# Macaron block with a gated delta-rule recurrence: the second half of the layers one group late, in halves of 256 tokens, inside the next group's recurrence

## What is computed

```python
x = x + 0.5 * ffn0(layernorm(x))          # silu(x wg) * (x wu), times wd; hidden width 768
x = x + delta_attention(layernorm(x))     # 16 heads, key width 64, value width 128
x = x + 0.5 * ffn0(layernorm(x))
x = x + 0.5 * shift_ffn(layernorm(x))     # mixes each token with the one before it
x = x + block_attention(layernorm(x))     # 16 heads of 16, causal inside blocks of 64 tokens
x = x + 0.5 * shift_ffn(layernorm(x))
# delta_attention, per head and token t, after projections, a causal convolution of 4 taps and silu:
S = a_t * (S - b_t * k_t (k_t S)) + k_t v_t ;  o_t = S q_t
# then an RMS norm of o_t and the product with Wo
```

## Time and profile before

| | us |
|---|---|
| median of 3 runs (9527.74 to 9530.57) | 9528.12 |
| the profiled execution, its time | 9529.48 |
| its span | 9527.7 |
| TensorE busy | 7091.6 (74%) |
| VectorE busy | 4742.1 (50%) |
| GpSimd busy | 2896.9 (30%) |
| ScalarE busy | 2594.3 (27%) |
| mean granted TensorE clock | 0.846 of 2.4 GHz |

### The profile page before, as it was taken

How to read it: one execution, slowest core, us unless ns; L and a number is a source line. 1 busy time by engine, 2 the same in 40 slices (tenths; PEclk the granted TensorE clock), 3 DMA queues, 4 the chain that set the end, 5 groups by cost and what they waited for, 6 DMA issues and landing times. The chain is left out here.

```text
span 9527.7 us, 151688 instructions
## 1 busy us (share of the span) xinstructions
PE 7091.6 (74%) x55840; PEld 4885.9 (51%) x55840; DVE 4742.1 (50%) x9325; ACT 2594.3 (27%) x5122; POOL 2896.9 (30%) x3781
## 2 busy tenths in 40 slices
PE   6777777767787777877778777787777777777777
PEld 3644546445464454645546455464554645546455
DVE  5445454454544545445454454545545455464553
ACT  2223132231322313223132231322313223132231
POOL 2315133251322513225132251322513225132251
PEclk8888888888888888888888888888888888888888
DMA  1101001010010100101001010010100101001010
GB/s 48 48 3 25 30 10 48 3 27 28 10 48 3 29 26 10 48 3 34 21 10 48 3 34 21 10 48 3 34 21 10 48 3 34 21 10 48 3 35 3
DMA packets 376009, 225.64 MB, mean 24 GB/s; under 512 B 336880, under 2 KB 353392, under 8 KB 366960
## 3 DMA queue, kind: packets, MB, share of 16 engines
q1 hardware_dynamic: 375152, 214.71, 7.5%
HBM read 155.95 MB, written 58.72 MB: 23 GB/s over the span
## 5 line engine op out<-in xcount | busy, mean ns | idle before, releaser
L538 DVE SCALAR_TENSOR_TENSOR SC<-SC,CW 128x512 f32<-128x512 f32 x1536 | 1281.9, 835 | 255.8 <-DVEq L536 170.0
L1097 PE MATMUL PS<-CST,SC 128*128 128x128 f32 x2432 | 494.7, 351 | 951.8 <-PEq L1105 520.2
L768 POOL TENSOR_TENSOR RSTD<-VAR,NHALF 128x2 f32<-128x2 f32 x192 | 133.8, 697 | 3009.0 <-POOLq L767 3009.0
L1097 PEld LDWEIGHTS PS<-CST,SC 128*128 128x128 f32 x2432 | 351.1, 177 | 1227.1 <-issue 1210.4
L839 POOL TENSOR_TENSOR WO<-WO 128x30 f32<-128x30 f32 (+14 forms) x960 | 581.9, 606 | 262.9 <-POOLq L853 126.3
L1094 PE MATMUL PS<-S,KQ 64*64 64x128 f32 x8192 | 659.2, 278 | 0.0
L842 POOL TENSOR_TENSOR WO<-WO 128x30 f32<-128x30 f32 (+14 forms) x960 | 613.8, 639 | 136.4
L1094 PE MATMUL PS<-XT,WV 128*128 128x512 f32 x1024 | 524.7, 652 | 115.0 <-PEq L1205 77.1
L862 POOL TENSOR_TENSOR FR<-MS,NHALF 128x8 f32<-128x8 f32 x128 | 210.0, 1641 | 1265.7 <-POOLq L861 1265.7
L1094 PE MATMUL PS<-XT,WQK 128*128 128x512 f32 x1024 | 576.2, 699 | 0.0
L1094 PE MATMUL PS<-WV,SC 64*64 64x128 f32 x8192 | 531.8, 280 | 41.9 <-PEq L1296 41.9
(11 more groups left out here) (159 smaller groups left out, 13423.5 us busy)
## 6 DMA issues: line engine op xcount, KB each, us to landing
WV<-in_wv SPq DMA_DIRECT2D x16, 2048.0 KB, 12.8
WO<-in_wo SPq DMA_DIRECT2D x16, 2048.0 KB, 7.5
WQK<-in_wq SPq DMA_DIRECT2D x16, 1024.0 KB, 4.8
WQK<-in_wk SPq DMA_DIRECT2D x16, 1024.0 KB, 6.9
cells_in<-SC SPq DMA_DIRECT2D x128, 128.0 KB, 2.8
WO<-cells_in SPq DMA_DIRECT2D x32, 512.0 KB, 3.3
cells_out<-WO SPq DMA_DIRECT2D x32, 512.0 KB, 2.6
cells_nat<-WO SPq DMA_DIRECT2D x32, 512.0 KB, 3.6
```

What stands on the lines that cost most here:

```text
L538: op = v.scalar_tensor_tensor(y, pre[:, j:j + G], CW[:, i * TAPS + j:i * TAPS + j + 1], y, ALU.mult, ALU.add)
L768: q.tensor_tensor(out=RSTD[:, 2 * k:2 * k + 2], in0=VAR[:, 2 * k:2 * k + 2], in1=NHALF[:, 0:2], op=ALU.pow).then_inc(rstd_ready, 1)
L1097: return nc.tensor.matmul(out_, in_, ident, is_transpose=True, start=True, stop=True)
```

## The change

The layers after the output projection become a generator, `tail`, on each of the four engines. It has 56 steps, marked by `yield`. They hold the layers of a whole group in two halves of HG = 256 tokens: feed-forward of both halves, first shift layer, attention of half 0, attention of half 1, second shift layer. `recurrence` of group n steps through the tail of group n - 1: 4 steps ahead of the first inverse (`FILL_FIRST`), then six in each of the 8 chunks in pairs A, B and C (`FILL`), then twice two. TensorE takes A behind `old_state` and the first `output_t`, B behind the second `output`, C behind `keys_t`. VectorE takes A and B between `right_side` and `s_update`, and C behind `mean_square`, ahead of `normalise`. GpSimd takes A and B with five columns of `substitute` behind each in chunks 0 to 2, C behind the power. ScalarE takes A ahead of the copies of `solve`'s result. The tail of group 0's recurrence works on a buffer of zeros, and the last group's tail is emitted by itself at the end.

The tail uses three PSUM banks (5 to 7) in a ring: each product claims the next (`claim` waits until its last reader has released it). The recurrence keeps banks 0 to 4; the transposed keys, `output_t`, the second inverse and the output projection (now one tile of 128 tokens at a time, `projected`, in chunks 5 to 7 and at the end) share bank 2. The second inverse is spread over chunks 3 and 4 in four passes, and two places of the first one wait for both copies together.

In attention the weights are no longer divided by their sum on GpSimd; `scaled` on VectorE divides the weighted sums. Two x buffers (`XS`) alternate, so VectorE's body and SyncE's loop now hold two groups. SyncE stores the late group when its tail ends and waits for the store, then loads the next x into the same buffer, then the projection weights, which before were loaded behind `chunks_done` and ahead of the rest. `chunks_done` now comes from the last tile of the output projection. The first feed-forward's layer norms take both statistics ahead of both normalisations.

```diff
+TAIL_STEPS = 56
+FILL_FIRST = 4
+FILL = 2
+
+
+def tail_ring():
+
+    order = ["x0f", "x1f"]
+    order += [f"g0{m}" for m in range(HT)] + ["d0"]
+    for m in range(HT):
+        order += [f"g1{m}"] + (["x0s"] if m == 3 else [])
+    order += ["d1", "r0s", "k0s", "v0s", "x1s", "r1s", "k1s", "v1s", "x0a"]
+    for h in range(2):
+        order += [f"q{h}0", f"q{h}1", f"va{h}", ("x1a", "x0u")[h], f"vd{h}0", f"vd{h}1", f"kt{h}0", f"kt{h}1", f"sc{h}0", f"sc{h}1"]
+        for i in range(4):
+            order += [f"pt{h}{i}", f"av{h}{i}"] + ([f"sc{h}{i + 2}"] if i < 2 else [])
+        order += [f"oa{h}", f"ao{h}"]
+    order += ["r0u", "k0u", "v0u", "x1u", "r1u", "k1u", "v1u"]
+    return {name: i % 3 for i, name in enumerate(order)}, order
+
+
+RING, RING_ORDER = tail_ring()
...
+        XB = sb("XB", 2 * NT * D)
+        XS = [XB[:, k * NT * D:(k + 1) * NT * D] for k in range(2)]
...
                     sp.dma_start(out[bass.ds(row + k * 2 * P, 2 * P), :].rearrange("(t p) d -> p t d", p=P),
-                                 v3(X[:, 2 * D * k:2 * D * k + 2 * D], 2)).then_inc(stored, 16)
+                                 v3(XS[p][:, 2 * D * k:2 * D * k + 2 * D], 2)).then_inc(stored, 16)
...
 
             def load_qkv():
                 for dst, src in ((WQ, wq), (WK, wk), (WV[:, :], wv)):
@@ -372,62 +408,67 @@
                 sp.wait_ge(a_done, 1)
                 sp.sem_inc(a_done, -1)
                 sp.dma_start(WO[:, :], wo).then_inc(wo_back, 16)
+
+            def next_qkv():
                 sp.wait_ge(chunks_done, 1)
                 sp.sem_inc(chunks_done, -1)
+                load_qkv()
...
+            load(G, 1)
+            next_qkv()
+            with sp.Fori(0, B * GROUPS // 2 - 1) as n:
+                for p in range(2):
+                    inverse_traffic()
+                    store(n * (2 * G) + p * G, p)
+                    load(n * (2 * G) + (p + 2) * G, p)
+                    next_qkv()
...
+                def hidden(h, m):
+                    ps, free = ring(f"g{h}{m}")
+                    s, u = m % 2, m % 3
+                    dve.wait_ge(tth_ready, 1)
+                    dve.sem_inc(tth_ready, -1)
+                    v.scalar_tensor_tensor(TTMP[:, s * HG:s * HG + HG], TTH[:, u * HG:u * HG + HG], 1.0, ps[:, 0:HG],
+                                           ALU.add, ALU.mult)
+                    dve.drain()
+                    v.tensor_tensor(out=THH[:, m * HG:m * HG + HG], in0=TTMP[:, s * HG:s * HG + HG], in1=ps[:, HG:G],
+                                    op=ALU.mult).then_inc(free, 1)
+                    if m == HT - 1:
+                        dve.drain().then_inc(hh_ready, 1)
+
+                def down(h):
...
+                def soft(h, i):
+                    ps, free = ring(f"sc{h}{i}")
+                    s = v3(SCB[i % 2], HB)
+                    dve.wait_ge(sc_ps, 1)
+                    dve.sem_inc(sc_ps, -1)
+                    v.tensor_tensor(out=s, in0=v3(ps, HB), in1=over(cst("amask"), HB, BLK), op=ALU.add).then_inc(free, 1)
+                    dve.drain()
+                    v.tensor_reduce(AMX[:, :], s, AX, ALU.max)
+                    dve.drain()
+                    v.tensor_tensor(out=s, in0=s, in1=each(AMX[:, :], HB, BLK), op=ALU.subtract).then_inc(sc_ready, 1)
+                    dve.drain()
+
...
+                for m in range(HT):
+                    hidden(0, m)
+                    yield
+                down(0)
+                yield
+                for m in range(HT):
+                    hidden(1, m)
+                    if m == 1:
+                        normal(0, x, TXN, txn_ready)
+                    if m == HT - 1:
+                        mix(0, 0)
+                    yield
+                down(1)
+                yield
+                normal(1, x, TXN, txn_ready)
+                yield
+                values(0, 0)
+                mix(1, 0)
+                yield
+                normal(0, x, TXN, txn_ready)
+                yield
+                values(1, 0)
+                yield
+                for h in range(2):
+                    rotate(h, 0)
+                    rotate(h, 1)
+                    if h == 0:
+                        normal(1, x, TXN, txn_ready)
+                    yield
+                    if h == 1:
+                        normal(0, x, TXN, txn_ready)
+                    yield
+                    spread(h, 0)
+                    spread(h, 1)
+                    yield
+                    yield
+                    soft(h, 0)
+                    yield
+                    soft(h, 1)
+                    sums(0)
+                    yield
+                    yield
+                    scaled(h, 0)
+                    soft(h, 2)
+                    sums(1)
+                    yield
+                    yield
+                    scaled(h, 1)
+                    soft(h, 3)
+                    sums(2)
...
+            def recurrence(p):
...
+                fill(FILL_FIRST)
                 keys(0)
...
-                        s_update(c, 1)
+                for c in range(CHUNKS):
+                    right_side(c, 0)
+                    right_side(c, 1)
+                    fill(FILL)
+                    fill(FILL)
+                    if c >= 5:
+                        projected(c - 5, XS[p])
+                    s_update(c, 0)
+                    s_update(c, 1)
...
+                    fill(FILL)
+                    if c >= 1:
+                        normalise(c - 1, 0)
+                        normalise(c - 1, 1)
+                fill(FILL)
+                fill(FILL)
+                mean_square(CHUNKS - 1)
+                normalise(CHUNKS - 1, 0)
+                normalise(CHUNKS - 1, 1)
+                projected(NT - 1, XS[p])
+                dve.drain()
 
...
+                    pool.sem_inc(qkt_ready, -1)
+                    masked_keys(0)
+                    masked_keys(1)
+                    yield
+                    yield
+                    masked_keys(2)
+                    yield
+                    yield
...
+                fill(FILL_FIRST)
                 pool.wait_ge(m_loaded, 16)
                 pool.sem_inc(m_loaded, -16)
-                cuts = (1, 14, 22, SUB - 1)
-                for c in range(CHUNKS):
-                    if c < 3:
-                        substitute(cuts[c], cuts[c + 1])
...
+                    for k in range(2):
+                        fill(FILL)
+                        if c < 3:
+                            substitute(1 + 10 * c + 5 * k, 6 + 10 * c + 5 * k)
...
+                    if c >= 1:
+                        pool.wait_ge(ms_ready, 1)
+                        pool.sem_inc(ms_ready, -1)
+                        q.tensor_tensor(out=FR[:, :], in0=MS[:, :], in1=NHALF[:, :], op=ALU.pow).then_inc(fr_ready, 1)
+                    if c < CHUNKS:
+                        fill(FILL)
 
...
+                    ps, free = ring(f"k{h}{'su'[n]}")
                     act.wait_ge(k_ps, 1)
                     act.sem_inc(k_ps, -1)
-                    ka = KA[:, k * G:k * G + G]
-                    a.activation(ka, bank(2 + k), ACT.Relu)
+                    a.activation(KA, ps, ACT.Relu).then_inc(free, 1)
                     act.drain()
-                    a.activation(ka, ka, ACT.Square).then_inc(ka_ready, 1)
+                    a.activation(KA, KA, ACT.Square).then_inc(ka_ready, 1)
...
+                def claim(name):
+                    ps, free = ring(name)
+                    if name not in RING_ORDER[0:3]:
+                        pe.wait_ge(free, 1)
+                        pe.sem_inc(free, -1)
+                    return ps
+
...
+
+                yield
+                transposed("x0f")
+                transposed("x1f")
+                yield
+                pe.wait_ge(txt_ready, 2)
+                pe.sem_inc(txt_ready, -2)
+                for m in range(HT):
+                    gate_up(0, m)
+                    yield
+                down(0)
+                yield
+                for m in range(HT):
+                    gate_up(1, m)
+                    if m == 3:
+                        transposed("x0s")
+                    yield
...
+                        ps = claim(f"kt{h}{k}")
+                        for j in range(2):
+                            for t in range(2):
+                                i = tr(ps[:, j * HG + t * P:j * HG + t * P + P], QKR[:, t * G + (2 * k + j) * P:t * G + (2 * k + j) * P + P])
+                        i.then_inc(qkt_ps, 1)
+                    yield
+                    scores(h, 0)
+                    yield
+                    scores(h, 1)
+                    yield
+                    weights_t(h, 0)
+                    yield
+                    weighted(h, 0)
+                    scores(h, 2)
+                    yield
+                    weights_t(h, 1)
+                    yield
+                    weighted(h, 1)
+                    scores(h, 3)
...
```

(93 more changed lines are left out.)

1191 lines of the change are left out of this document (682 added, 509 removed).

## The result

The changed kernel takes 9195.58 us (median of 4 runs, 9192.0 to 9202.95) against 9527.93 (9522.26 to 9530.57, 4 runs): ratio 0.9653, interval 0.9636 to 0.967. It is faster, by 3.5%. The forecast was 8892, 6.7% faster; the time lies inside the range of 8490 to 9350, 304 us above the point, between the forecast and rival (b).

The account below looks back on a forecast made before the run. TensorE was taken to bound the stretches where it is fed, handoffs the others. From a span of 9527.7 us, 833 saved over 16 groups and 195 added for the last group's lone tail gave 8890, so 8892 executed; range 8490 to 9350.

Parts of the forecast that it names:

- (b): Rival: VectorE comes late at each chunk's boundary, 3 us more a chunk, 24 a group, 9276 us; chance 0.17.
- merged stretch: Part of a group where recurrence and the late group's tail run interleaved; forecast 291 us, from 227, 54 and 10.
- front: A group's first feed-forward, projections and decay matrices; 248 us, its order left nearly alone by the change.
- waits: TensorE's waits when both streams run in its one order, counted chunk by chunk from entry to exit: 54 us a group.
- boundary: Loop overhead between groups: about 2.2 us, against 3.3 before, since one boundary of two loses its loop.
- The tail that runs alone: The last group's tail, in halves with handoffs exposed, at the end: 195 us, bounds 174 and 230.
- floor of 227: TensorE's work from recurrence through last shift layer, summed at the upper clock: 227 us a group.
- cold restarts: Lower-clock loss at a colder start, behind chunk 3's wait and at the last projection: 10 us a group.
- masked keys in chunk 6: TensorE's scores wait there for GpSimd's masked keys: 2.0 us of chunk 6's 3.9, named among the largest.
- (a): Rival: waits are mostly absorbed and the clock stays up, 29 to 32 us a group less, 8430 us; chance 0.16.
- 3 us nor 10: VectorE's slowdown beside GpSimd's substitution: 3 us, or some 10 a group if the shared port's loser fully blocks.
- (c): Rival: interrupted TensorE gets the lower clock as in attention, 98 us lost instead of 10, 10300 us; chance 0.09.

Follow-up runs that it names:

- e1_block: Changed kernel with all 56 tail steps ahead of the first inverse, so the tail is not interleaved: 10329.1 us.
- e3_warm: Changed kernel plus 46 idle TensorE products a group in front of waits for the normalised output and the returned inverse: 9088.7 us.
- e10_idle_mixed: Changed kernel plus 64 idle products a group, one ahead of each 64-row pair of a half solve: 9825.8 us.
- e5_order: Changed kernel with seven feed-forward and attention steps swapped so TensorE has other ready work before its waits: 9114.1 us.
- e4_nosub: Changed kernel without GpSimd's substitution of the second half, so the second inverse is not the inverse: 9084.6 us.
- e2_norm: Changed kernel with VectorE normalising the finished chunk between the two tail steps of pair C instead of behind both: 9208.7 us.
- e12_three_exit: Changed kernel with seven steps swapped, VectorE's exit order moved, GpSimd's slices recut, and 14 idle products at the exit only: 8985.9 us.
- e8_three_warm: Changed kernel with seven steps swapped, VectorE's exit order moved, GpSimd's slices recut, and 36 idle products a group before waits: 9020.1 us.

## Why the prediction was right or wrong

**The bound and the direction** were right, and the time lies in the range. TensorE's busy time is about what it was (7044.5 against 7091.6 us), and filling one stream's idle time with the other's work is what gains, as e1_block shows by taking it away: two thirds of its effect is idle time, one third the higher clock that comes with it. But of the prediction's own signs of being wrong one came up: TensorE's work in the merged stretch is 251.1 us, well over the 240 it named, and the granted clock 0.91, not over 0.93.

**The sum**, term by term for one group: front 247.2 against 248 (right); waits 59.1 against 54; TensorE's busy time 251.1 against 237; boundary 3.5 against 2.2. Together 561 against 541.2. Sixteen times the 20.2 us between the stores is 323. The tail that runs alone is 179 us by the method that gave 174 before, from the end of the last projection, at 8999.9, to the end of the last add at 9179.5; I had 195, so 16 us come back. 323 - 16 = 307 of the 304 us. The row of the end:

```profile
8991.03 8.88 PE L1403 MATMUL PS<-WO,VO 128*128 128x256 f32 x32 [0.87 <-PEq L1809]
```

**The mis-sized term** is TensorE's time in the merged stretch, 251 us against 237, 14 us a group; the other terms came out within 5 us. It was added up from a floor of 227 and 10 for cold restarts, three to six of them. The 10 is what failed. In this group there are nine stretches at the lower clock level, of 3.4 to 10.2 us; the last two of them and the sum of all nine:

```profile
3348.90:3355.70 6.80, 5.93 (x16) 4.97 (x17) 1.97 (x5) 1.19 (x2) 0.00 (x0) 0.50 0.01 2
3376.20:3386.40 10.20, 5.63 (x16) 4.29 (x17) 1.29 (x2) 1.20 (x2) 1.64 (x1) 0.50 0.29 89
sum 58.40, PE 48.43 PEld 41.59 DVE 15.46 ACT 11.03 POOL 10.73; mean PE 5.38 PEld 4.62 DVE 1.72 ACT 1.23 POOL 1.19
```

TensorE is busy for 48.4 of these 58.4 us. If each product takes twice its time there, 24 us are lost, 14 more than the 10, and 251.1 less 24 is the floor of 227. Over all 16 groups the mean is 249.7 us busy, 45.8 of them at the lower level. The 24 is an upper estimate, since not every product doubles (64 records of 32 x 32 take 1.73 us at 3198.40 and 1.20 at 3210.70). e3_warm supports it: the same method gives 26.4 us a group at the lower level there instead of 45.8, so some 10 us a group given back, for 21 us of idle products put mostly into waits.

The floor left out a second thing, going from one form to the other. There are 26 places of two tail steps in the merged stretch; at 0.19 us a round trip, the rows of chunk 0, they would cost 5 us, and at 0.34, e10_idle_mixed's row, 9. The clock leaves no room for 9: with its 24 us nothing is left to explain. So the change of form costs between nothing and some 5 us a group in this kernel, and these runs don't say more closely. The prediction also read 0.216 us a record off the output projection, whose own row (29.91 us for 128) gives 0.234; in the merged stretch the four projections take 30.3 us against the 27.7 of the floor, most of it in the last one, which runs in part at the lower level. Two slips had no effect: the lone tail's bound of 230 gives 9359, not 9350, as the top of the range, and attention's loss by the clock is 43% of its work (58.7 against 41), not 40.

**The waits** came out at 59 against 54, with the largest where they were named: the exit's 5.66 and 6.24, and in chunk 3 the returned blocks (L1857) and the copy of the inverse's first product (L1892):

```profile
3187.96 3.23 PE L1403 MATMUL PS<-S,KQ 64*64 64x128 f32 x32
...
3198.40 1.73 PE L1403 MATMUL PS<-WO,SC 32*32 32x32 f32 x64 [3.67 <-PEq L1857]
...
3217.27 1.15 PE L1403 MATMUL PS<-CST,KQ 64*64 64x64 f32 x32 [3.47 <-PEq L1892]
```

Chunk by chunk they are as near: entry 5.1 us against 5.1, chunk 1 2.4 against 2.0, chunk 2 7.7 against 7.3, chunk 3 8.1 against 7.5, chunk 4 4.8 against 4.9, chunk 7 5.6 against 5.4, exit 17.8 against 16. Two missed: the wait for the masked keys in chunk 6, named as one of the largest, is in no row of the merged stretch (1.8 us in all in that chunk against 3.9), and chunk 5 has 5.8 against 2.2, with 1.9 for the rows of a layer norm and 1.6 for the normalised output. No wait in the merged stretch passed 10 us. That the handoffs of adjacent steps cost time on the path, against rival (a), e5_order shows: 81 us off for reordering them alone. Such waits could be taken away by order, which I had not asked: the exit and the seven steps together were 9.8 of the 54 us.

**GpSimd.** I charged the second inverse 7.5 us in chunk 3. e4_nosub puts the whole price of the substitution at 6.9 us a group, spread beyond chunk 3. As to the shared port, VectorE's work of the merged stretch is 140.6 us (I had some 160, against 138 before), so neither 3 us nor 10 can be read out of it; leaving the substitution out took VectorE's busy time over the span only from 4897.7 to 4882.5 us, 1 us a group. In the merged stretch the rows give no sign of whole instructions blocked. In the front they do, once in each of the 16 groups: a VectorE operation with two SBUF operands that takes 0.75 us otherwise starts just behind GpSimd's copy of 1.94 us and takes 2.43, ending 0.55 us behind it. The two rows of the changed kernel:

```profile
3071.16 1.94 POOL L1055 COPY WO<-WO 128x1024 f32<-128x1024 f32 x1
...
3071.22 2.43 DVE L750 SCALAR_TENSOR_TENSOR SC<-SC,CW 128x512 f32<-128x512 f32 x1
```

The kernel before has the same (2.45 us at 2643.27). Beside the second half's copy, at 3184.82, VectorE works on operands from PSUM and takes its usual 0.69 us.

**The rivals.** (a) fell by the waits. (b) was not the mechanism: its 24 us a group were to come from VectorE being late, but only 5 us more are waits. e2_norm shows that VectorE's order is a trade, not slack. The time is nearer to (b)'s 9276 (80 us off) than to the forecast, for another reason than (b)'s, the clock. (c), the lower clock throughout, did not happen: the whole merged stretch is granted 0.91. Its rule, of the Trainium skill's page TensorE: Matmul & The Clock Gate (A second HAM failure mode: psum-queue depth-cycling), on cycling banks with small idles, is borne out in part. Chunks 1, 2 and 7 of the merged stretch, in the table of stretches:

```profile
3123.30:3150.90 27.60, 25.20 (x261) 21.89 (x260) 15.48 (x44) 5.18 (x11) 14.88 (x22) 1.00 0.01 2
3150.90:3188.00 37.10, 29.41 (x279) 23.69 (x278) 23.04 (x60) 8.81 (x15) 14.75 (x26) 1.00 0.01 4
3313.20:3344.00 30.80, 25.25 (x254) 21.88 (x252) 11.72 (x32) 5.77 (x10) 1.86 (x2) 0.89 0.00 1
```

All three cycle the same banks. Chunk 1 is idle for 2.4 us and chunk 2 for 7.7, with a wait of 3.04 us, and both keep the upper level to their end; chunk 7, idle for 5.6 us with no wait over 2.69, doesn't. So the lower level does follow small idles here, behind chunk 2 as well (3188.5 to 3191.9), but neither their sum in a chunk nor the longest of them says where.

**Hidden as said**: the x load, the weights' load and VectorE's total. **Not foreseen**: the boundary's longer gap; what makes it longer was not tried.

## What to carry to other kernels

When two streams are merged on TensorE, the floor added up from rows at the upper clock level and the list of waits, one by one, can both be right (227 us, and 59 against 54) and the sum still short: what failed here was the time lost at the lower level, up to 24 us a group where 10 were given. Here there were nine cold stretches a group where three to six restarts had been counted. The change of form, 0.1 to 0.17 us each, is the smaller item. Then ask of each wait whether the engine that waits has something ready to do first; moving the engine that delivers only moved the wait. Where nothing is ready, idle products pay if the stretch behind the wait ran cold and if the wait is longer than they are, which has to be read again after each other change: here the same 14 products gained 45 us where they stood alone, and 11 us with 22 more further up.

## What was not expected of the hardware

- Going between full-array and 64-row products costs about 0.1 us each way between long runs, and 0.17 when it happens at every pair (2.05 us for 12 changes).
- Idle products in front of a 5.66 us wait halved the shift product behind it (3.62 to 1.89 us), but 12 before the last projection left it at 8.83 us (e3_warm), while 2 before it went with 7.14 us in e12_three_exit and 8.83 in e8_three_warm.
- A VectorE operation of 0.75 us took 2.43 when it started beside a GpSimd copy of 1.94 us and both its operands lay in SBUF.
- With two groups instead of one in the loop's body, VectorE's gap at the loop's turn grew from 2.78 to 5.52 us.
